# A four-layer transformer kernel: fewer Vector operations per chunk step in the second layer's delta attention, and the third layer's cosine attention written as one interleaved pass

## What is computed

```
def step(S, inp):
    q_t, k_t, v_t, beta_t, alpha_t = inp
    S = S * alpha_t[..., None, None]
    kv = jnp.einsum('bhk,bhkv->bhv', k_t, S)
    S = S + jnp.einsum('bhk,bhv->bhkv', k_t, (v_t - kv) * beta_t[..., None])
    o_t = jnp.einsum('bhk,bhkv->bhv', q_t, S)
    return (S, o_t)
...
o = o * lax.rsqrt(mean(o*o) + EPS) * norm_w
o = o * (z * jax.nn.sigmoid(z))
out = jnp.einsum('btv,hv->bth', o.reshape(b_, t_, VAL_DIM), out_w)
```

```
norms = jnp.linalg.norm(x, axis=-1)
dots = jnp.einsum('bil,bjl->bij', x, x)
sim = dots / jnp.maximum(norms[:, :, None] * norms[:, None, :], EPS)
atten = jax.nn.softmax(sim, axis=-1)
out = jnp.einsum('bij,bjl->bil', atten, x) + x
```

## Time and profile before

| what | value |
|---|---|
| median of 3 runs | 8202.75 us (8200.53 to 8206.14) |
| the profiled execution | 8215.13 us |
| its span, first to last instruction | 8213.4 us |
| PE busy | 6890.2 us (84%) |
| DVE busy | 5947.1 us (72%) |
| ACT busy | 4031.0 us (49%) |
| POOL busy | 2784.7 us (34%) |
| mean granted TensorE clock | 0.883 |

### The profile page before, as it was taken

One profiled execution on the slowest core, in us unless ns is written; L12 is line 12 of the kernel. 1 busy time (PEld: TensorE's weight loads), 2 busy tenths in 40 slices (PEclk: granted clock), 3 DMA queues, 4 the chain that ended last, 5 costly groups with the idle time before them and its releaser, 6 DMA issues. The chain is left out here.

```text
span 8213.4 us, 272064 instructions
## 1 busy us (share of the span) xinstructions
PE 6890.2 (84%) x118760; PEld 4856.6 (59%) x118760; DVE 5947.1 (72%) x10595; ACT 4031.0 (49%) x6820; POOL 2784.7 (34%) x1918
## 2 busy tenths in 40 slices
PE   7999789999997998998998998998997689445566
PEld 3444478888886665665665665665665455334434
DVE  6666379999996895885895995985996567842366
ACT  3555245555553775775775775774774212210121
POOL 0101023333332773773773773773771000011000
PEclk8999589999998999999999999999998789555556
DMA  0000000000000221221221221221220000000000
GB/s 15 1 1 1 1 5 6 4 4 4 4 3 23 69 74 41 73 71 44 71 73 42 70 74 41 74 71 44 71 73 17 11 6 2 3 3 4 5 0 13
DMA packets 187948, 249.07 MB, mean 30 GB/s; under 512 B 58997, under 2 KB 85492, under 8 KB 185844
## 3 DMA queue, kind: packets, MB, share of 16 engines
q1 hardware_dynamic: 186740, 231.40, 10.8%
HBM read 27.84 MB, written 2.10 MB: 4 GB/s over the span
## 5 line engine op out<-in xcount | busy, mean ns | idle before, releaser
L1771 PE MATMUL wa_front<-w_wqkv,wa_xT 128*128 128x512 f32 x1920 | 951.2, 619 | 27.7 <-ACT wa_qT L1764 11.1
L1699 POOL TENSOR_TENSOR XNT<-XNT 128x1024 f32<-128x1024 f32 x384 | 907.2, 2363 | 145.8 <-DVE XNT L1869 145.8
L1702 POOL TENSOR_TENSOR XNT<-XNT,wa_rnorm 128x1024 f32<-128x1024 f32 x320 | 608.8, 1902 | 448.4 <-DVE wa_rnorm L1877 447.0
L1771 PEld LDWEIGHTS wa_front<-w_wqkv,wa_xT 128*128 128x128 f32 x1920 | 337.3, 196 | 299.8 <-issue 261.6
L446 PE MATMUL a0h_ring<-a0h_QT,a0h_KT 32*128 32x512 f32 (+3 forms) x1536 | 464.5, 577 | 14.2 <-ACT a0h_E L564 10.4
L564 ACT ACTIVATE a0h_E<-a0h_ring 128x512 f32<-128x512 f32 (+1 forms) x640 | 320.4, 555 | 304.9 <-PE a0h_ring L446 303.3
L1866 DVE TENSOR_TENSOR XNT<-wa_front,w_scaled 128x1024 f32<-128x1024 f32 x320 | 380.5, 1189 | 84.5 <-PE wa_front L1771 83.8
L1777 PE MATMUL wa_front<-consts,XNT 128*128 128x128 f32 x2560 | 359.8, 285 | 74.0 <-POOL XNT L1702 72.0
L1777 PEld LDWEIGHTS wa_front<-consts,XNT 128*128 128x128 f32 x2560 | 284.6, 144 | 228.1 <-POOL XNT L1702 199.2
L1869 DVE TENSOR_TENSOR XNT<-wa_front,w_scaled 128x512 f32<-128x512 f32 x640 | 408.7, 680 | 0.0
L1882 DVE TENSOR_REDUCE wa_norm<-wa_sq 128x16 f32<-128x1024 f32 x320 | 368.0, 1185 | 14.7 <-ACT wa_sq L1717 14.1
(11 more groups left out here) (624 smaller groups left out, 17987.8 us busy)
## 6 DMA issues: line engine op xcount, KB each, us to landing
wa_v_look<-wa_v_all SPq DMA_DIRECT2D x960, 128.0 KB, 2.4
wa_v_look<-wa_v_all SPq DMA_DIRECT2D x640, 64.0 KB, 2.1
wal_v_look<-wal_v_all SPq DMA_DIRECT2D x192, 128.0 KB, 2.4
wal_v_look<-wal_v_all SPq DMA_DIRECT2D x128, 64.0 KB, 2.1
w_wqkv<-in_L_ffn_Wqkv_dram SPq DMA_DIRECT2D x6, 1024.0 KB, 6.4
w_wo<-in_L_ffn_Wo_dram SPq DMA_DIRECT2D x6, 512.0 KB, 6.9
w_wqkv<-in_L_ffn_Wqkv_dram SPq DMA_DIRECT2D x12, 256.0 KB, 8.0
f2w_raw<-in_L_ffn_w_dram SPq DMA_DIRECT2D x48, 64.0 KB, 1.9
```

Source lines behind the costliest of these rows:

```text
L1699: g.tensor_tensor(rot[:, at], rot[:, at], part[:, at], ALU.add).then_inc(s[summed], 1)
L1702: g.tensor_tensor(rot[:, at], rot[:, at], spread(rnorm[:, at, :], HDW), ALU.mult).then_inc(s[done], 1)
L1771: last = pe.matmul(front[:, first + i, :], x_of(which), wqkv[:, (2 * n + i) * 512:(2 * n + i + 1) * 512], start=True, stop=True)
```

## The change

In the delta stage: (1) the multiplication of `y` by `rstd` is gone. The four parts of the output are scaled by `rstd` as they are added to X, by four 128x128 operations in place of one of 128x512, and `y` is ready at the gating product. (2) `place` is gone from DVE. One GpSimd product of `XTc`, repeated along the columns, with the mask `head_blocks` writes the diagonal blocks and the zeros around them. (3) The two level operations on GpSimd are one, and `sb` stands ahead of it. DVE's `XTc` now waits for all levels.

In the cosine stage the loop is written out. All batch entries go through one block: the tiles of `dots` of one entry alternate with the tiles of `out` of the entry before it. The norms of entry 0 are taken by DVE, those of 1 and 2 by GpSimd products and DVE sums, those of 3 by ACT. The row of inverse norms of the next entry is made in slots 3 (DVE) and 5 (PE, ACT) of the present one. GpSimd adds XN to X ahead of time, so that DVE has one addition for each tile, and PE reads XNT with no copy.

```diff
@@ delta_chunk_steps, gpsimd
+                if j is not None:
+                    if j >= 1:
+                        g.wait_ge(s["strict_ready"], j)
+                    g.tensor_tensor(sb[:], c.strict.unsqueeze(1).broadcast_to(four),
+                                    spread(of_chunk(nb_all[:], j), P), ALU.mult).then_inc(s["sb_ready"], 1)
                 if q is not None:
                     g.wait_ge(s["Nc_ready"], q + 1)
...
-                    g.tensor_tensor(lev[:, 0], Nc[:], small[:, 0:1, :].broadcast_to(tiny), ALU.mult).then_inc(s["lev0_ready"], 1)
-                    g.tensor_tensor(lev[:, 1:SMALL], Nc[:].unsqueeze(1).broadcast_to([P, SMALL - 1, G, 32]),
-                                    small[:, 1:SMALL, :].unsqueeze(2).broadcast_to([P, SMALL - 1, G, 32]),
+                    g.tensor_tensor(lev[:], Nc[:].unsqueeze(1).broadcast_to([P, SMALL, G, 32]),
+                                    small[:, 0:SMALL, :].unsqueeze(2).broadcast_to([P, SMALL, G, 32]),
                                     ALU.mult).then_inc(s["lev_ready"], 1)
...
+                    g.wait_ge(s["X_ready"], LD * (q + 1))
+                    g.tensor_tensor(XT[:, q % 2].rearrange("p b (k x) -> p b k x", x=32),
+                                    XTc[:].unsqueeze(2).broadcast_to([P, G, 4, 32]),
+                                    c.head_blocks.rearrange("p (k x) -> p k x", x=32).unsqueeze(1).broadcast_to([P, G, 4, 32]),
+                                    ALU.mult).then_inc(s["x4_ready"], 1)
@@ vector
-                    v.wait_ge(s["lev0_ready"], q + 1)
+                    v.wait_ge(s["lev_ready"], q + 1)
+                    if q >= 1:
+                        v.wait_ge(s["x4_ready"], q)
                     v.tensor_tensor(XTc[:], lev[:, 0], ident, ALU.add).then_inc(s["X_ready"], 1)
...
                     v.wait_ge(s["out_ps"], e + 1)
+                    v.wait_ge(s["rstd_ready"], e + 1)
                     mine = X[:].rearrange("p (b t) d -> p b t d", b=G)[:, :, e % BLOCKS, :]
-                    v.tensor_tensor(mine, bank[4][:], mine, ALU.add).then_inc(s["added"], 1)
+                    for b in range(G):
+                        last = v.scalar_tensor_tensor(out=mine[:, b], in0=bank[4][:, b, :], scalar=rstd[:, b:b + 1],
+                                                      in1=mine[:, b], op0=ALU.mult, op1=ALU.add)
+                    last.then_inc(s["added"], 1)
...
-                    v.tensor_tensor(y[:], o[:], gatez[:, r % 2], ALU.mult)
+                    v.tensor_tensor(y[:], o[:], gatez[:, r % 2], ALU.mult).then_inc(s["y_ready"], 1)
...
-                if q is not None:
-                    place()
...
-                    chain(v.reciprocal(rstd[:], std[:]))
-                    v.tensor_tensor(y[:], y[:], spread(rstd[:], P), ALU.mult).then_inc(s["y_ready"], 1)
+                    v.reciprocal(rstd[:], std[:]).then_inc(s["rstd_ready"], 1)
@@ l2_attention_stage, written anew (the loop over b is gone)
+            def _(g):
+                g.memset(xv[:, :, P:P + 1], 1.0).then_inc(s["ones_set"], 1)
+                g.tensor_copy(xv[:, 0:BLOCKS, 0:P], XN[:, 0:BLOCKS, :]).then_inc(s["xv_ready"], 1)
+                for b in range(1, LAST):
+                    g.tensor_tensor(squares[:, b], of_batch(XN, b), of_batch(XN, b), ALU.mult).then_inc(s["squared"], 1)
+                for b in range(BATCH):
+                    if b >= 1:
+                        g.tensor_copy(xv[:, b * BLOCKS:(b + 1) * BLOCKS, 0:P], of_batch(XN, b)).then_inc(s["xv_ready"], 1)
+                    g.tensor_tensor(of_batch(X, b), of_batch(X, b), of_batch(XN, b), ALU.add).then_inc(s["base_ready"], 1)
...
+            def _(v):
...
+                v.tensor_tensor(diag[:], XN[:, 0:BLOCKS, :], XN[:, 0:BLOCKS, :], ALU.mult).then_inc(s["norm2_first"], 1)
+                v.wait_ge(s["norm2_first"], 1)
+                v.tensor_reduce(of_batch(norm2, 0), diag[:], AX.X, ALU.add).then_inc(s["norm2_first"], 1)
+                invert(slice(0, BLOCKS), "norm_first", 0)
+                diagonals(0)
...
+                for b in range(BATCH):
                     for t in range(BLOCKS):
+                        n = b * BLOCKS + t
+                        if n > BLOCKS:
+                            finish(n - BLOCKS - 1)
+                        v.wait_ge(s["rrow_ready"], b + 1)
+                        v.tensor_scalar(scale[:, n % 2, :], rrow[:, b % 2, :], rnorm[:, n:n + 1], 1.0 / COS_EPS,
+                                        ALU.mult, ALU.min).then_inc(s["scale_ready"], 1)
...
+                        if n >= 2:
+                            v.wait_ge(s["exps"], n - 1)
+                        v.tensor_tensor(sim[:, n % 2, :], dots[:, n % 2, :], scale[:, n % 2, :],
                                         ALU.mult).then_inc(s["sim_ready"], 1)
...
+                        if t == DIAG_SLOT and b < LAST:
+                            diagonals(b + 1)
...
+            def _(pe):
...
+                for b in range(BATCH):
                     for t in range(BLOCKS):
+                        similar(b * BLOCKS + t)
+                        if b >= 1:
+                            weigh((b - 1) * BLOCKS + t)
+                        if t == ROW_SLOT and b < LAST:
+                            row(b + 1)
+                for t in range(BLOCKS):
+                    weigh(LAST * BLOCKS + t)
```

More of the change, by code:

```diff
@@ L1387, in grow @@
                     v.transpose(flat(T[:]), flat(XTc[:])).then_inc(s["T_ready"], 1)
-                def place():
-                    for k in range(4):
-                        last = v.tensor_copy(XT[quarter(k), slot, :, quarter(k)], XTc[quarter(k)])
-                    last.then_inc(s["x4_ready"], 1)
                 if q is not None:
@@ L2165, in l2_attention_stage @@
     with Stage(nc, "a2") as st:
[L2166 to L2169 removed]
+        xv = st.sb("xv", [P, TILES, P + 1])
+        squares = st.sb("squares", [P, BATCH - 1, BLOCKS, P])
+        norm2, norm, rnorm = (st.sb(n, [P, TILES]) for n in ("norm2", "norm", "rnorm"))
+        rtotal = st.sb("rtotal", [P, 2])
@@ L2170, in l2_attention_stage @@
         diag = st.sb("diag", [P, BLOCKS, P])
-        rrow = st.sb("rrow", [P, SEQ])
+        rrow = st.sb("rrow", [P, 2, SEQ])
         scale = st.sb("scale", [P, 2, SEQ])
         sim = st.sb("sim", [P, 2, SEQ])
-        E = st.sb("E", [P, BLOCKS, SEQ])
-        mean = st.sb("mean", [P, 2, P])
-        wide = st.ps("wide", (P, 2, SEQ))
+        E = st.sb("E", [P, 2, BLOCKS, SEQ])
+        dots = st.ps("dots", (P, 2, SEQ))
+        rows = st.ps("rows", (P, SEQ))
         out = st.ps("out", (P, 2, 512))
-        s = st.sems("xs_ready xv_ready norm2_ready norm_ready diag_ready row_ready rrow_done dots_ready sim_ready "
-                    "exps out_ready out_used added ones_set chain")
@@ L2256, in l2_attention_stage, with finish @@
-            st.end_step()
+                def finish(n):
+                    v.wait_ge(s["out_ready"], n + 1)
+                    v.reciprocal(rtotal[:, n % 2:n % 2 + 1], out[:, n % 2, P:P + 1]).then_inc(s["rtotal_ready"], 1)
+                    v.wait_ge(s["rtotal_ready"], n + 1)
+                    v.wait_ge(s["base_ready"], n // BLOCKS + 1)
+                    v.scalar_tensor_tensor(out=X[:, n, :], in0=out[:, n % 2, 0:P], scalar=rtotal[:, n % 2:n % 2 + 1],
+                                           in1=X[:, n, :], op0=ALU.mult, op1=ALU.add).then_inc(s["added"], 1)
@@ new lines, in _ @@
+                v.tensor_tensor(diag[:], XN[:, 0:BLOCKS, :], XN[:, 0:BLOCKS, :], ALU.mult).then_inc(s["norm2_first"], 1)
[3 more added lines that the diff above has]
+                diagonals(0)
+                for b in range(1, LAST):
+                    v.wait_ge(s["squared"], b)
+                    v.tensor_reduce(of_batch(norm2, b), squares[:, b], AX.X, ALU.add).then_inc(s["norm2_rest"], 1)
@@ new lines, in _, with row, similar, weigh @@
+                for n in range(TILES - BLOCKS - 1, TILES):
+                    finish(n)
+                v.wait_ge(s["added"], TILES)
+            @block.tensor
+            def _(pe):
+                def row(b):
+                    pe.wait_ge(s["diag_ready"], b + 1)
+                    if b >= 1:
+                        pe.wait_ge(s["rrow_ready"], b)
+                    for k in range(2):
+                        last = pe.matmul(rows[:, k * 512:(k + 1) * 512], c.ones,
+                                         diag[:, 4 * k:4 * k + 4, :].rearrange("p t n -> p (t n)"), start=True, stop=True)
+                    last.then_inc(s["row_ready"], 1)
+                def similar(n):
+                    b, t = n // BLOCKS, n % BLOCKS
+                    mine = XNT[:, b * SEQ:(b + 1) * SEQ]
+                    if n >= 2:
+                        pe.wait_ge(s["sim_ready"], n - 1)
+                    for k in range(2):
+                        last = pe.matmul(dots[:, n % 2, k * 512:(k + 1) * 512], mine[:, t * P:(t + 1) * P],
```

(27 more changed lines are left out.)

123 lines of the change are left out of this document (47 added, 76 removed).

## The result

| | median us (runs) | against before, on the same chip |
|---|---|---|
| kernel before | 8204.44 (8200.53 to 8224.58, 4 runs) | |
| changed kernel | 8116.53 (8110.30 to 8135.00, 4 runs) | ratio 0.9892, 95% interval 0.9869 to 0.9914: -88 us, between -71 and -107 |
| changed kernel, second set | 8139.8 (8117.52 to 8149.73, 5 runs) | before 8206.16 (11 runs); ratio 0.9924, 0.9907 to 0.9941: -62 us, between -48 and -76 |

The forecast was 8146, 57 us less than before. In the second set one execution of six, at 15165 us, is left out. The two profiled executions differ by 104.8 us of span (8213.4 and 8108.6), so the first task is to see where those lie. The traces were cut at the same instructions: the first `ga` of the delta stage, its last addition to X, GpSimd's first operation of the cosine stage, its last addition to X; each cut is where the named instruction starts.

What follows compares the result with a forecast made beforehand. PE was taken to pace most of the delta step, with DVE's stretch up to T level; cosine iterations waited in a line. Delta -20 and cosine -37 from the 8202.75 median gave 8146 us, range 8114 to 8180.

Steps and rivals of the forecast that it cites:

- Scaling at the addition: Delta stage: T comes 0.7 us sooner, four additions cost 0.55 more than one, leaving 0.15 us a step.
- Placing on GpSimd: Delta stage: DVE's copies become a GpSimd product, so `tx(5)` starts 0.18 us sooner each step.
- Levels: Delta stage: one level product with `sb` ahead of it, counted as nothing; bounds -0.3 to +0.3 us a step.
- Delta stage: Scaling and placing together give 0.33 us a step over 62 full steps: -20 us, bounds -39 to +12.
- Rival 2: Delta stage gives nothing, T at `zt(3)` coming where it came: 8166 us; chance 0.24.
- rival 3: Delta stage: GpSimd's order becomes the chain and the kernel gets slower, 8239 us with T 1.5 late; chance 0.03.
- Cosine stage: Whole cosine stage falls from 183.2 to 146.1 us, -37, bounds -52 and -30; first `scale` at 25.7.
- rival 1: Cosine stage: diagonals pass in one run without taking turns, first `scale` at 13.5, stage -49, 8134 us; chance 0.26.
- a late start: Cosine prologue: about 1.2 us until DVE's square of 1024 columns lets GpSimd start.
- rival 4: Cosine stage: the overlap doesn't come, since `out` waits for DVE's finishes, 8183 us; chance 0.07.
- The tail: End of the cosine stage: 8 x 1.78 = 14.2 us of `out` and 0.8.
- The total: Whole kernel: -20 and -37 make -57 us, from a median of 8202.75 to 8146; chance 0.40.

Runs made afterwards that it cites:

- d_scale: Kernel before with only the rstd multiplication of y dropped and the output scaled at its addition to X: step 23.61 us, delta stage 1547.2, one run of 8205.41 us.

## Why the prediction was right, and where its sizes were off

- **Scaling at the addition: 0.15 expected, 0.31 measured.** The first half held: T 0.73 sooner against 0.7, in the changed kernel and in `d_scale`. The price of the four additions was too high: "I take 3 x 0.28 + 0.35 = 1.2", so 0.55 more than the one. What the one addition held DVE for is the time from its start at 19.91 to the next start, in the trace of before:

```profile
1720.48 0.68 DVE L1423 TENSOR_TENSOR a1s_u<-a1s_bank,a_beta_all 128x512 f32<-128x512 f32 x1
```

  From 19.91 to 20.48 are 0.57, and the four hold it for 1.00: +0.43, and 0.73 - 0.43 = 0.30. The working had both too high, the one by 0.08 (its duration of 0.65, whose end overlaps with what follows) and the four by 0.20 (they start 0.25 apart, though each lasts a third of a microsecond). The Trainium skill's overhead of 125 ns per DVE instruction on PSUM ("Perfetto Trace Analysis", section Optimizing Scalar/DVE Operations) gave an estimate of 0.38 for three more instructions and of a gain of 0.32. The trace shows 0.43 / 3 = 0.14 each and a gain of 0.31: the page was nearer than my pick.
- **Placing on GpSimd: 0.18 expected, 0.22 measured**, by the mechanism named: `tx(5)` waits for ACT alone, 0.21 less. The Trainium skill's "so offloading operations between those two might not help" ("Perfetto Trace Analysis", the same section) was the case against. The trace bears out the shared port (1.63 for a convolution that takes 0.75 alone) and not the consequence: the held operation is one that nobody waits for.
- **Levels: 0 expected, +0.03 measured.** The reason given also held; T waits for whichever of `ga` and the level product comes last.
- **Delta stage:** -20 expected, -28.8 and -29.2 measured. A step of 23.6 was announced and 23.40 found; 9 of the miss lies here. The sum took 62 equal steps. The 14 steps with L1017 gain 0.14 only, a term that the working had at nothing: PE's slack ahead of `y` had hidden that work, and the change removed the slack. That cost some 5 us. The parts that were priced too low gave 0.19 a step more than the sum, some 12 us, so the stage still gained more than was forecast. Rival 2 (nothing gained) and rival 3 (GpSimd's order becomes the chain) are both refuted by the step. In the step of the earlier trace rows GpSimd waited 2.52 for `Nc` (the 1.63 of the working are from an early step):

```profile
1717.40 0.86 POOL L1328 TENSOR_TENSOR a1s_lev<-a1s_Nc,a_small 128x128 f32<-128x128 f32 x1 [2.52 <-ACT a1s_Nc L1256]
```

  With `sb` in between, which takes 1.05, it still waits 0.63 in most steps and 1.01 in the one shown, which has L1017, so `sb` did not make the levels late.
- **Cosine stage:** -37 expected, -38.6 and -40.1 measured. The diagonals did take turns, so rival 1 falls: 13.76 us against "some 14". The first `scale` came 23.1 after the start against 25.7. The ten GpSimd operations and DVE's eight were through 18.1 after the start, against some 21. The turns that I added for the diagonals, 8 x 0.2, did not show: GpSimd's operations follow one another without a gap. The 1.2 for a late start did show, as a first copy of 2.10 where the later ones take 1.03. The two squares took 1.89 each and not 2.36, which gives back 0.9. So the 18.1 are near the 18.3 for GpSimd's own ten by chance: two errors of about 1 us cancel. The rows and their eviction behind the diagonals took 5.0 against 4.5. From the first `out` to the last exponential 85.7 + 0.6 were expected and 6407.52 - 6320.75 = 86.8 found, with PE setting the pace, so rival 4 falls too. The tail was 15.1 against 15.0, to the end of the last addition.
- **The total:** -57 expected. The touched stages gave -67 and -69, the timed sets -88 and -62. Of the 29.5 us between 8146 and the first median, 10.4 are these two terms (67.4 - 57). The rest lies in code that did not change. The range of 8114 to 8180 was made from the touched stages alone and held both medians. The second lies well inside. That the first does too, by 2.5 us, is luck, since nothing in the working allowed for other stages to change by 37 us. By the touched stages alone the time would be 8202.75 - 67.4 = 8135, and there the mechanism is what was forecast.

## What to carry to other kernels

Price a group of short operations by what it adds until the next start on its engine, not by durations end to end. When DVE and GpSimd both have work queued, ask which operations of the two are on the path and put GpSimd's unhurried ones (here four additions and three copies) behind a count that keeps them off that stretch: that was worth 10 to 11 us in one stage. When a change removes a wait, look for work that runs only now and then and that the wait had hidden: here 0.39 us in 14 of 62 steps. A difference between two traces is to be cut by stage first, since unchanged stages can carry a third of it.
